# An adaLN-style two-layer FFN on one core: base weight in its natural column order, LoRA B read with a stride

## The reference, cut to what matters

```python
# condition: a 1x1 convolution with a mix of 8 experts per batch
agg_w = einsum('bk,koi->boi', att, weight)
y = einsum('boi,bih->boh', agg_w, x) + (att @ bias_k)[:, :, None]
# feed-forward: a base product and two low-rank ones (8 groups of 256 rows)
base_out = y @ kernel + bias                        # 1024 x 1024
Ax   = einsum('bri,bti->btr', A_eff, y)             # A_eff, B_eff: gated LoRA, rank 32
delta = einsum('bor,btr->bto', B_eff, Ax) + einsum('or,btr->bto', lora_B_shared, Ax_s)
x = x + base_out + delta
# second layer: a grouped convolution of 9 taps, a SwiGLU feed-forward, x = x + ...
```

## Time and profile before

| what | value |
|---|---|
| median of 3 runs (lowest, highest) | 789.18 us (788.33, 790.32) |
| profiled execution: its own time | 788.27 us |
| its span | 786.5 us |
| granted TensorE clock, mean | 1.00 of full speed |
| TensorE busy | 775.0 us |
| VectorE, ACT, POOL busy | 523.2, 216.1, 79.7 us |
| prologue (until the first base product) | 0 to 22.6 us |
| base stage | until 266.5 us |

### The profile page before, as it was taken

The page is one execution under the profiler, slowest core; times in us unless marked ns, Lnnn a source line. Parts: engine busy times, 40 slices in busy tenths (PEclk is TensorE's granted clock), DMA queues, the critical chain, the costliest instruction groups (busy, mean ns, idle before and its releaser), DMA issues.

```text
span 786.5 us, 10467 instructions
## 1 busy us (share of the span) xinstructions
PE 775.0 (99%) x3933; PEld 657.0 (84%) x3933; DVE 523.2 (67%) x624; ACT 216.1 (27%) x254; POOL 79.7 (10%) x54
## 2 busy tenths in 40 slices
PE   7999999999999999999999999999999999999998
PEld 6898788888888999978888888888888888888886
DVE  4866953453545679977777769777755896555552
ACT  5740110010010114143333336333333731111110
POOL 3240623224223000000000000000000000000000
PEclk9999999999999999999999999999999999999999
DMA  8969644464585997445553042388752854444441
GB/s 230 308 216 269 177 108 129 115 150 112 119 194 156 206 249 200 134 119 144 141 140 103 27 187 81 126 238 237 234 209 80 301 197 171 160 161 165 164 172 59
DMA packets 90772, 131.47 MB, mean 167 GB/s; under 512 B 10952, under 2 KB 70200, under 8 KB 88048
## 3 DMA queue, kind: packets, MB, share of 16 engines
q1 hardware_dynamic: 87808, 129.67, 56.4%
q10 hardware_dynamic: 2752, 1.12, 0.5%
q0 software_dynamic: 176, 0.21, 0.1%
HBM read 79.24 MB, written 51.72 MB: 167 GB/s over the span
## 4 chain that ended last, share of the span: by engine, by line
PE 93%; DMA 2%; DVE 2%; SPq 1%; issue 1%; ACT 1%; DVEq 0%
PE ps L1877 38%; PE ps L1619 37%; PE ps L1937 18%; DMA raw<-in_L_ffn_kernel 2%; DMA h_f<-h_scratch 1%; DVE wk_lo L1080 1%; SPq L398 0%; DVE res L1548 0%; ACT wk_hi L816 0%; ACT w_s_hi L899 0%; DVE y_lo L1138 0%; DVE w_a_lo L1281 0%; DVE la_lo L1075 0%; SPq L393 0%; DVE w_s_lo L1271 0%
## 5 line engine op out<-in xcount | busy, mean ns | idle before, releaser
L1877 PE MATMUL ps<-cr,w_s_hi 128*128 128x512 f32 x512 | 157.5, 389 | 0.0
L1877 PE MATMUL ps<-cr,w_a_hi 128*128 128x512 f32 x384 | 118.3, 390 | 1.1 <-DVE s L1400 1.1
L1877 PEld LDWEIGHTS ps<-cr,w_s_hi 128*128 128x128 f32 x512 | 96.1, 188 | 20.0
L1877 PE MATMUL ps<-cr,w_s_lo 128*128 128x512 f32 x256 | 99.6, 389 | 0.0
L1877 PEld LDWEIGHTS ps<-cr,w_a_hi 128*128 128x128 f32 x384 | 71.9, 188 | 16.3 <-issue 1.5
L1619 PE MATMUL ps<-wk_hi,y_hi 128*128 128x512 f32 x256 | 80.6, 396 | 1.0 <-DVE la_lo L1075 0.9
L1619 PE MATMUL ps<-wk_lo,y_hi 128*128 128x512 f32 x256 | 79.0, 390 | 0.0
L1619 PE MATMUL ps<-wk_hi,y_lo 128*128 128x512 f32 x256 | 78.8, 389 | 0.0
L752 POOL TENSOR_TENSOR x_t<-x_in,f_bias 128x1024 f32<-128x1024 f32 x16 | 63.0, 3935 | 147.1 <-DMA x_scratch<-x_t 136.5
L1163 DVE TENSOR_TENSOR x_t<-ps,x_t 128x1024 f32<-128x1024 f32 x16 | 19.5, 1222 | 86.9 <-PE ps L1619 86.9
L1877 PE MATMUL ps<-cr,w_a_lo 128*128 128x512 f32 x192 | 74.7, 389 | 0.0
(11 more groups left out here) (185 smaller groups left out, 1245.6 us busy)
## 6 DMA issues: line engine op xcount, KB each, us to landing
x_scratch<-x_t SPq DMA_DIRECT2D x128, 64.5 KB, 2.2
x<-x_scratch SPq DMA_DIRECT2D x32, 258.0 KB, 6.9
x_in<-in_x SPq DMA_DIRECT2D x16, 512.0 KB, 5.1
r_scratch<-r_t SPq DMA_DIRECT2D x16, 512.0 KB, 3.2
h_scratch<-s SPq DMA_DIRECT2D x32, 256.0 KB, 2.4
h_f<-h_scratch SPq DMA_DIRECT2D x8, 1024.0 KB, 5.9
res<-r_scratch SPq DMA_DIRECT2D x16, 512.0 KB, 5.0
raw<-in_L_ffn_w SPq DMA_DIRECT2D x56, 128.0 KB, 4.5
```

The source lines that it names most:

```text
L1877: last = pe.matmul(o, l, r, start=first and q == 0 and n == 0, stop=q == 3 and n == 2, skip_group_check=True)
```

## The change

The base weight is split in its natural column order: wk_hi and wk_lo are read and written in one run of 1024. LoRA B keeps its order by fours in lb_1 and lb_2. The four LoRA products of a tile now read it in natural order: lb_columns gives for each half 128 values of c, and for each of them the four values of a, which lie 256 elements (1024 bytes) apart. The destination is the bank in order, written as (c a). take_x1 reads the banks as "p (b h q)", a step of 8 elements (32 bytes) between innermost elements; what it computes and writes is the same. The number and the order of instructions are the same on all engines, and so are the DMAs.

```diff
--- before.py
+++ after.py
@@ -335,13 +335,9 @@
 
             return lb_c[hl][:, :].rearrange("p (y q) -> p q y", q=NX)[:, 4 * n:4 * n + 4]
 
-        def by_quarter(tile):
-
-            return tile.rearrange("p (q c) -> p q c", q=OQ)
-
-        def in_quarters(tile):
-
-            return tile[:, :].rearrange("p (c q) -> p q c", q=OQ)
+        def lb_columns(tile, half):
+
+            return tile[:, :].rearrange("p (a c) -> p c a", a=OQ)[:, half * P:(half + 1) * P, :]
 
         def lbs_part(hl):
 
@@ -813,7 +809,7 @@
             def wk_hi_part(k):
 
                 act.wait_ge(raw_in[k % 4], 16 * (k // 4 + 1))
-                act.activation(by_quarter(wk_hi[:, k, :]), in_quarters(raw[k % 4]), ACT.Copy).then_inc(wk_hi_made, 1)
+                act.activation(wk_hi[:, k, :], raw[k % 4][:, :], ACT.Copy).then_inc(wk_hi_made, 1)
 
             def split_y(t, s, a):
 
@@ -1077,8 +1073,7 @@
 
             def wk_lo_part(k):
                 dve.wait_ge(wk_hi_made, k + 1)
-                dve.tensor_tensor(by_quarter(wk_lo[:, k, :]), in_quarters(raw[k % 4]), by_quarter(wk_hi[:, k, :]),
-                                  ALU.subtract).then_inc(wk_lo_made, 1)
+                dve.tensor_tensor(wk_lo[:, k, :], raw[k % 4][:, :], wk_hi[:, k, :], ALU.subtract).then_inc(wk_lo_made, 1)
                 dve.wait_ge(wk_lo_made, k + 1)
                 dve.sem_inc(raw_free, 1)
 
@@ -1160,7 +1155,7 @@
             def take_x1(t, s):
                 dve.wait_ge(u_mm, t + 5)
                 dve.wait_ge(xb_made, t + 1)
-                dve.tensor_tensor(blocks(x1_t[s]), bank(2 + 2 * s, 2).rearrange("p (q b h) -> p h q b", h=2, q=4),
+                dve.tensor_tensor(blocks(x1_t[s]), bank(2 + 2 * s, 2).rearrange("p (b h q) -> p h q b", h=2, q=4),
                                   blocks(x1_t[s]), ALU.add).then_inc(x1_made, 1)
 
             def lb_lo_part(n):
@@ -1745,7 +1740,7 @@
                 rows = slice(a * P, (a + 1) * P)
                 for z, b in ((z_1, lb_1), (z_2, lb_2)):
                     for half in range(2):
-                        last = mm(dst[half], z[s][:, rows], b[s][:, half * HALF:(half + 1) * HALF], False, b is lb_2)
+                        last = mm(dst[half].rearrange("p (c a) -> p c a", a=OQ), z[s][:, rows], lb_columns(b[s], half), False, b is lb_2)
                 last.then_inc(u_mm, 1)
 
             def first_u(a, k):
```

## The result

| | before | changed |
|---|---|---|
| median of 10 runs | 788.22 us | 790.47 us |
| profiled span | 786.5 us | 787.3 us |
| TensorE busy | 775.0 us | 778.2 us |
| VectorE, ACT busy | 523.2, 216.1 us | 518.6, 208.7 us |

The ratio is 1.0031, with a 95% interval of 1.0015 to 1.0046: 2.4 us slower, where 45 us were forecast and 797 us was the lowest time of the range. The forecast's direction holds, its size is wrong by a factor of about twenty.

A forecast was written before the change was run, and what follows sets the result against it. The prediction took TensorE to bound the base stage. From the profiled 788.27 us it took 0.9 for the splits, added 46.3 for the LoRA products and 0 for take_x1: 833.7 us, range 797 to 838.

The forecast's parts named there:

- What bounds the kernel: Base stage: TensorE is the bound, busy 775.0 of 786.5 us; work off VectorE or ACT gains only TensorE's waits.
- Part 1: Base weight splits, wk_hi and wk_lo: reading in one run removes TensorE's wait on la_lo, -0.9 us.
- next late is TensorE itself: After the la_lo wait goes: TensorE has work without a gap, so no more than 0.9 us to gain.
- Part 2: The 64 LoRA products: jumping reads cost 1.83 ns a column, 951 ns a product instead of 227, +46.3 us.
- rival (a): LoRA products at half rate: a jumping column takes about two TensorE steps, +13.7 us, 801.1 us; chance 0.27.
- The 14 ns that the prediction calls fixed: Each LoRA product: 227 ns start to start, taken as 213 ns for 512 columns plus 14 ns fixed.
- The estimate from that page in the prediction: LoRA products: 1.67 ns for each 16-byte line, 869 ns a product, 41 us for 64, 828.5 us in all.
- Part 3: take_x1 on VectorE: reading PSUM with a step of 32 bytes instead of 8 costs nothing, 0 us.
- (b): LoRA products not slower: TensorE's own reader fetches jumping columns at full pace, price zero, 787.4 us; chance 0.17.
- (c): LoRA products: price between half rate and forecast, say 813 us, or beyond it through a 1.2 GHz clock; chance 0.08.

The follow-up runs named there:

- lora_only: Kernel before, with only the 64 LoRA products reading by jumps, weight still split by quarters, take_x1 unchanged: 790.99 us, ratio 1.0047.
- all_by_jumps: Changed kernel, but weight split by quarters as before and all 768 base products also reading by jumps: 829.05 us, ratio 1.0526 to before.
- splits_only: Kernel before, with only the base weight split in natural order, LoRA products and take_x1 unchanged: 786.71 us, ratio 0.9989.
- the rulers: Three kernels whose LoRA products read 512 columns in another pattern from tile to tile, against one run at 227 ns: 215 to 541 ns a product.
- base_pairs: Against before: natural order, weight stored as even and odd halves, base and LoRA products reading two places in turn: 782.89 us, ratio 0.9926.
- all_pairs: base_pairs, with the gate and out stage products also reading two places in turn: 764.47 us, ratio 0.970.

## Why the prediction was wrong, point by point

**What bounds the kernel: right for what is added.** TensorE is the bound of the base stage; what its products cost more came out in the time, in lora_only and in all_by_jumps, and nothing hid it. What they cost less did not all come out: behind TensorE stand the transfer of LoRA B and the first wait of the gate stage.

**Part 1: the pieces and the wait right, what comes after it not.** The pieces cost what the rows of runs said, and the wait on la_lo went. The forecast took 0.9 us, the one wait in the list; TensorE gained 1.3 in the changed kernel. From start to start the products after that wait came 1.2 us sooner, since a wait is listed from the modelled end of the product before it and the first product after it is slower; and before, those of 29.19 us could start only when wk_lo of piece 2 ended (27.03 + 2.02 = 29.05), some 0.15 us, which shows in no wait of its own. But "next late is TensorE itself" is wrong: in splits_only LoRA B's transfer is late next, and took the gain back in that trace. The -0.9 us that its ratio gives (interval 0.1 to 1.7) can't be followed to the splits.

**Part 2: the step that failed.** The price of a jump was taken as "a price of the memory's port, not of the engine", because ACT and VectorE agree on 1.83 ns. TensorE pays (275 - 14) / 512 = 0.51 ns a column, 0.09 more than without jumps. The 46.3 us of the sum measured 3.1. Two things were wrong in it. First, that two engines agree says nothing of a third that reads in another way. Even where each column of TensorE needs a line of its own, with steps of 32 and 64 bytes, it needs 427 to 429 ns, 0.81 a column by the same sum, and in the dearest walk of all, sixteen places, 1.03; 1.83 was met nowhere. Second, "a jumping read" is not one kind of read. The rows of before show a uniform step, which never comes back to the 16 bytes that it has left; the change goes round four places and comes back to each after four columns. The prediction read the size of the jump (1024 bytes) and not the order in which the bytes are met again. By the rulers the size of the jump does not matter: two places in turn cost nothing at 16, 64, 1024, 2048 and 4096 bytes, four the same 275 ns at 1024 and 2048. Where a step was uniform, rival (a), the half rate with its 440 ns, would have been right to 4%. The 14 ns that the prediction calls fixed are not fixed either: two places in turn leave 2 of them.

The page "SBUF — State Buffer" of the Trainium skill, section "Door 1: The DMA port swizzle", in the note on cachelines, says that at least two hits in a line of 16 bytes are needed for full bandwidth. For TensorE the table agrees only if each of two readers is counted by itself: a step of 8 bytes has two hits in each line, and costs about 450 ns for 227. The estimate from that page in the prediction, 869 ns for a product, charged every column a whole line; measured are 275.

**Part 3: right.** take_x1 stays at 1223 ns with a step of 32 bytes.

**The rivals.** The result lies nearest to (b), with the price that (b) named as its limit: 48 ns measured against 37 ns. A reader of TensorE's own was the better picture; "no limit of reading" was not, since even one run costs 12 ns more than two places in turn. (c), the clock, did not happen in the changed kernel; it did in base_pairs and all_pairs, after a wait on VectorE. That the direction came out as forecast is no credit to the price: the 48 ns lie just above the 37 at which the prediction itself drew the line to no change. The range of 797 to 838 left out just the case that came, with a chance of 0.17.

## What to carry to other kernels

A price read on one engine is a price of that engine: for a third one it is a bound with a wide other end, and the range has to reach down to nothing as long as no row of its own speaks. For a moving operand of fp32r, count the places that the columns are taken from in turn, whatever their distance: two cost nothing, four with neighbours in each 21% (275 for 227 ns), eight or more over double, and a uniform step of 8 bytes or more about double. And before a gain on the bounding engine is counted, ask which transfer it meets next. Two runs read in turn are 5% faster than one run (215 for 227 ns at 512 columns), which gave 3% of this kernel for a change of views alone.

## What the runs showed of the hardware that was not expected

- TensorE reads two places in turn faster than one run, at every distance tried, and so runs at 512 columns in 215 to 216 ns; one run costs 227.
- Runs of two columns that jump (445 ns) cost more than single columns that do (275).
- Writing PSUM in pairs that jump 16 or 32 bytes costs nothing (215 to 216 ns with two places in turn and 16 bytes, 227 with one run and 32). The page "PSUM — Partial Sum Buffer" of the Trainium skill, section "Specifications (TRN2)", says that any non-contiguous pattern slows matmuls significantly; for pairs these runs show the opposite, and single columns that jump in PSUM were not measured.
- Waits of 2.0 and 2.1 us at the start of the gate stage were followed by a granted clock of 0.83 in that window of 10 us (base_pairs, all_pairs); waits of 1.1 to 1.8 us at the same place were not, nor was one of 3.2 us for LoRA B in the base stage.
